# A twelve-stage perceiver block on one core: one barrier at each stage's end, the fourth couple of experts fetched by SyncE, a root ahead on ScalarE

## What is computed

```python
x = x + _L0_xattn_ref(_layernorm(x), ctx_1024, ...)     # stage slots
x = x + _L0_attn_ref(_layernorm(x), ...)                # patt
x = x + _L0_ffn_ref(_layernorm(x), ...)                 # quant
x = x + _L1_xattn_ref(_layernorm(x), ctx_1024, ...)     # padded
x = x + _L1_attn_ref(_layernorm(x), Wqkv, bqkv, Wo, bo) # folded
x = x + _L1_ffn_ref(_layernorm(x), Wg, w1, w2)          # moe
x = x + _L2_xattn_ref(_layernorm(x), ctx_1024, ...)     # cross
x = x + _L2_attn_ref(...)  # delta    then _L2_ffn_ref   # local
x = x + _L3_xattn_ref(...) # plain    then _L3_attn_ref  # mqa
x = x + _L3_ffn_ref(...)   # hashed

def _L1_attn_ref(x, Wqkv, bqkv, Wo, bo):
    qkv = (x @ Wqkv.T + bqkv).reshape(B, 16, S, 3 * hd)
    ...
def _L1_ffn_ref(x, Wg, w1, w2):
    gate = softmax(xr @ Wg); idx = argmax(gate)
    h = relu(einsum('ecm,emf->ecf', dispatched, w1))
    expert_out = einsum('ecf,efm->ecm', h, w2)
    ...
```

## Time and profile before

| | |
|---|---|
| median of 3 runs | 1777.92 us (1773.97 to 1778.31) |
| the profiled execution | 1778.89 us |
| its span, first to last instruction | 1777.1 us |
| TensorE matmul busy | 1433.1 us (81%) |
| VectorE busy | 1001.7 us (56%) |
| ScalarE busy | 700.0 us (39%) |
| GpSimd busy | 96.5 us (5%) |
| mean DMA rate over the span | 102 GB/s |

### The profile page before, as it was taken

The page is one execution under the profiler, slowest core; times in us unless marked ns, Lnnn a source line. Parts: engine busy times, 40 slices in busy tenths (PEclk is TensorE's granted clock), DMA queues, the critical chain, the costliest instruction groups (busy, mean ns, idle before and its releaser), DMA issues. The chain is left out here.

```text
span 1777.1 us, 28179 instructions
## 1 busy us (share of the span) xinstructions
PE 1433.1 (81%) x10760; PEld 1067.2 (60%) x10760; DVE 1001.7 (56%) x2900; ACT 700.0 (39%) x1524; POOL 96.5 (5%) x90
## 2 busy tenths in 40 slices
PE   7999999776598447799999999999983654647975
PEld 6979889554376233367776777777762532445763
DVE  5645444584565312277777777777756945343333
ACT  5735445212121110167667667666761010112211
POOL 2300000000000210200000000001000000000000
PEclk9999999888799659799999999999996565658997
DMA  9944333100331749410000000000002007007810
GB/s 320 327 164 160 118 111 140 53 1 20 139 131 56 249 153 350 180 59 33 33 33 33 33 33 33 33 32 33 2 1 116 1 0 301 0 0 261 277 57 4
DMA packets 61783, 181.15 MB, mean 102 GB/s; under 512 B 7249, under 2 KB 41169, under 8 KB 60369
## 3 DMA queue, kind: packets, MB, share of 16 engines
q1 hardware_dynamic: 56864, 156.77, 24.7%
q0 software_dynamic: 4352, 16.78, 2.6%
q10 hardware_dynamic: 432, 5.80, 0.8%
HBM read 178.68 MB, written 0.66 MB: 101 GB/s over the span
## 5 line engine op out<-in xcount | busy, mean ns | idle before, releaser
L1733 ACT ACTIVATE cross_s<-cross_s,cross_shift 128x896 f32<-128x896 f32 x224 | 215.1, 1031 | 35.2 <-DVE cross_shift L1813 35.2
L1727 ACT COPY cross_eT<-cross_ring 128x512 f32<-128x512 f32 x280 | 153.2, 591 | 144.9 <-PE cross_ring L1653 144.9
L1653 PE MATMUL cross_ring<-consts,cross_s 128*128 128x128 f32 x1568 | 199.4, 280 | 8.7 <-ACT cross_s L1733 8.7
L1653 PEld LDWEIGHTS cross_ring<-consts,cross_s 128*128 128x128 f32 x1568 | 170.7, 142 | 59.1 <-issue 43.8
L1804 DVE CUSTOM_DVE_ANT_0 cross_s<-cross_scores,cross_mask,cross_top 128x448 f32<-128x448 f32 x224 | 141.3, 680 | 84.3 <-PE cross_scores L1645 84.3
L374 ACT ACTIVATE slots_probs<-slots_scores,slots_bias,ctx_rinv 128x128 f32<-128x128 f32 x294 | 130.2, 460 | 109.0 <-DVE slots_bias L418 109.0
L1804 DVE CUSTOM_DVE_ANT_0 cross_s<-cross_scores,cross_mask,cross_half_max 128x448 f32<-128x448 f32 x224 | 141.3, 681 | 18.8 <-PE cross_scores L1645 18.8
L134 PE MATMUL slots_scores<-slots_qkT,slots_ctxT 128*128 128x128 f32 x1176 | 139.8, 277 | 9.1 <-DMA slots_ctxT<-in_ctxT 8.2
L134 PEld LDWEIGHTS slots_scores<-slots_qkT,slots_ctxT 128*128 128x128 f32 x1176 | 138.3, 194 | 13.0 <-DMA slots_ctxT<-in_ctxT 9.2
L324 PE MATMUL slots_attended<-ctx_rows,slots_probs 128*128 128x257 f32 x588 | 135.2, 380 | 1.4 <-DVE slots_pooled L432 1.4
L1645 PE MATMUL cross_scores<-cross_keysT,cross_qz 32*128 32x448 f32 x896 | 119.0, 589 | 0.8 <-DVE cross_keysT L1778 0.8
(11 more groups left out here) (742 smaller groups left out, 2114.3 us busy)
## 6 DMA issues: line engine op xcount, KB each, us to landing
slots_ctxT<-in_ctxT SPq DMA_DIRECT2D x42, 896.0 KB, 4.6
ctx_rows<-in_ctx_rows SPq DMA_DIRECT2D x28, 896.0 KB, 7.6
padded_ctxT<-in_ctxT SPq DMA_DIRECT2D x14, 896.0 KB, 4.6
cross_ctxT<-in_ctxT SPq DMA_DIRECT2D x14, 896.0 KB, 4.6
plain_ctxT<-in_ctxT SPq DMA_DIRECT2D x14, 896.0 KB, 4.7
ring_w<-in_moe_w POOLq DMA_DIRECT2D x12, 1024.0 KB, 17.8
ring_w<-in_moe_w SPq DMA_DIRECT2D x12, 1024.0 KB, 11.8
local_layers<-in_w_local SPq DMA_DIRECT2D x2, 4806.0 KB, 15.3
```

What stands on the lines that cost most here:

```text
L1653: last = pe.transpose(bank(("turn", u, t))[:, j * P:(j + 1) * P], s_buf[:, u % 2, j, t * P:(t + 1) * P], K.ident)
L1727: act.copy(eT[:, u % 2, t], bank(item)).then_inc(st("emptied_act"), 1)
L1733: act.activation(rows, rows, ACT.Exp, bias=shift[:, u % 2, j:j + 1], scale=SCALE).then_inc(st("exp"), 1)
```

## The change

Four edits.

- `Stage.__exit__` no longer has the second barrier. GpSimd clears the stage's semaphores while the others go on. To keep that safe, every new semaphore takes a number that is not among those just cleared (`semaphore`, `Stage.cleared`). The numbers a stage gets then lie in more than one run, so the clearing at its end is one to four instructions where it was one.
- GpSimd fetches couples 0 to 2 in the folded stage, and no longer waits for `o2_in`.
- SyncE fetches couple 3 as its first work in the moe stage.
- `root_table` is put at the end of ScalarE's list in every stage but hashed: a square root of one column of the constants into `K.unused`, which nobody reads. The load of the table with the root thus stands at the end of a stage and no longer at the start of the next.

```diff
+def semaphore(nc, name):
+    num = next(n for n in nc.free_semaphores if n not in Stage.cleared)
+    return nc.alloc_semaphore(name=name, num=num)
 class Stage:
+    cleared = []
...
-            self.sems[name] = self.nc.alloc_semaphore(name=f"{self.name}_{name}")
+            self.sems[name] = semaphore(self.nc, f"{self.name}_{name}")
...
-            self.nc.clear_and_free_semaphores(list(self.sems.values()))
-            self.nc.all_engine_barrier()
+            mine = list(self.sems.values())
+            Stage.cleared = [s.num for s in mine]
+            self.nc.clear_and_free_semaphores(mine)
...
+def root_table(act, K):
+    act.activation(K.unused, K.ident[:, 0:1], ACT.Sqrt)
...
                 softmax_scalar(act, st, "f", ef[:, :], D ** -0.5)
+                root_table(act, K)
...
             def _(pool):
                 pool.wait_ge(st("folded_in"), 16)
-                for p in range(SLOTS):
-                    if p == SLOTS - 1:
-                        pool.wait_ge(st("o2_in"), 16)
+                for p in range(SLOTS - 1):
                     K.ring.fetch_w1(pool, p)
                     K.ring.fetch_w2(pool, p)
...
             def _(sp):
+                K.ring.fetch_w1(sp, SLOTS - 1)
+                K.ring.fetch_w2(sp, SLOTS - 1)
                 for p in range(SLOTS, COUPLES):
                     sp.wait_ge(st("hid_mm"), p - SLOTS + 1)
                     K.ring.fetch_w1(sp, p)
```

More of the change, by code:

```diff
@@ L76, in __init__ @@
         self.T, self.region = T, region
-        self.arrived = {n: nc.alloc_semaphore(name=f"arrived_{n}") for n in HOMES}
+        self.arrived = {n: semaphore(nc, f"arrived_{n}") for n in HOMES}
     def buf(self, name):
@@ L946, in scalar @@
                 exponentials(g)
+        root_table(act, self.K)
     def vector(self, dve):
@@ L1251, in __init__ @@
         self.w2 = [w2[:, s] for s in range(SLOTS - 1)] + [second]
-        self.w1_in = [nc.alloc_semaphore(name=f"w1_in{n}") for n in range(2 * SLOTS)]
-        self.w2_in = [nc.alloc_semaphore(name=f"w2_in{n}") for n in range(2 * SLOTS)]
+        self.w1_in = [semaphore(nc, f"w1_in{n}") for n in range(2 * SLOTS)]
+        self.w2_in = [semaphore(nc, f"w2_in{n}") for n in range(2 * SLOTS)]
     def turn(self, p):
@@ L2225, in __init__ @@
         self.T, self.rotary, self.layers = T, rotary, layers
-        self.arrived = [nc.alloc_semaphore(name=f"arrived_local{n}") for n in range(LAYERS)]
+        self.arrived = [semaphore(nc, f"arrived_local{n}") for n in range(LAYERS)]
     def fetch(self, eng, n):
@@ L2747, in perceiver @@
         K = Kept()
-        out_written = nc.alloc_semaphore(name="out_written")
+        out_written = semaphore(nc, "out_written")
         K.x = sb("x_kept", [P, D])[:, :]
@@ L2753, in perceiver @@
         K.idle = consts[:, 0:2 * P]
+        K.unused = sb("unused", [P, 1])[:, :]
         with Stage(nc, "first") as st:
```

2 lines of the change are left out of this document (1 added, 1 removed).

## The result

| | before | change |
|---|---|---|
| median | 1775.95 us (1773.39 to 1778.31, 4 runs) | 1751.39 us (1749.61 to 1752.29, 4 runs) |
| profiled execution | 1778.89 us | 1752.29 us |
| its span | 1777.1 us | 1750.2 us |

The ratio is 0.9861, 95% interval 0.9842 to 0.9880. In the changed kernel's numbering L161 is L169, L165 is L173, L172 is L180, L1144 is L1161, L1261 and L1265 are L1277 and L1281, L1362 is L1381, L789 and L819 are L805 and L835.

A forecast was written before the change was run, and what follows sets the result against it. TensorE binds the long stages; the change touches only seams, where VectorE waits 28.7 us on the second barrier. 10.7 + 7.5 + 1.6 = 19.8 us off 1778.9 gives 1759.1 us, range 1752 to 1766.

The forecast's parts named there:

- Couple 3, 10.7 us: Folded's end: GpSimd's drain waits for its own couple 3 transfers; moving them to SyncE takes 10.7 us off.
- Both covers: In moe: couple 3 lands 14 us before TensorE wants it; SyncE is free for couple 4 with 4 us left.
- couple 3 again: Rival in moe: SyncE's four transfers delay couple 4, costing up to the 11 us gained: 1769.8, chance 0.06.
- the drain by itself: Rival at folded's end: GpSimd's DRAIN is long without waiting for transfers, so 10.7 us stay: 1769.8, chance 0.05.
- The barrier, 7.5 us: Stage ends: one barrier less, 14 times, saves 8.2 us less most of quant's part: 7.5 us.
- The first rival: Stage starts: the second barrier hid the next block's start; 3.8 us stay (1762.9), or all (1766.6); chance 0.16.
- The root, 1.6 us: Starts of folded, delta, mqa and hashed: no table load ahead of the root saves 0.39 us each, 1.6 us.
- clock can equally fall sooner somewhere: Unknown: TensorE's clock may drop earlier in some stage, losing a like amount to the 2.4 us possible in moe.
- the reading by the row: Quant: the library load runs from MODIFY_POOL_CONFIG, 7.6 us to the first call, so quant gains only 0.1 us.
- the rival's 1.1 us: Quant: load counted from L819's end, gaining 1.1 us more; in the rival "more than the sum", 1755.6, chance 0.12.
- the list of unknowns: Two unknowns: what the second barrier covered (0 to 8.2 us gained) and TensorE's clock at moe's start (0 to 2.4).
- The whole stretch at full clock, 2.4 us: Moe's start: TensorE's clock may rise sooner after a shorter pause, gaining up to 2.4 us; nothing was counted.

The follow-up runs named there:

- e1: The kernel before with only couple 3's fetch moved from GpSimd to SyncE: 1761.93 us, ratio 0.9911.
- e2: The kernel before with one barrier a stage end in place of two and the semaphores' numbers chosen as in the change: 1767.66 us, ratio 0.9937.
- e3: The kernel before with only the unused root added in ten stages, its buffer keeping all addresses modulo 64: 1772.76 us, ratio 0.9968.
- e14: The changed kernel with GpSimd's library loaded in patt and the weights' fourth place moved 184 bytes, to 0 modulo 256: 1745.44 us, ratio 0.9822.
- e0: The kernel before, unchanged, against itself: 1776.22 us against 1776.43, ratio 0.9997.
- e9: The changed kernel with GpSimd's library loaded in patt by one unused PARTITION_ALL_REDUCE: 1744.28 us, ratio 0.9818.
- e10: The kernel before with an unused buffer of 96 bytes a partition, ring_w at 64 modulo 128: 1776.38 us in one execution.
- e13: The kernel before with an unused buffer of 160 bytes a partition, ring_w at 128 modulo 256: 1774.69 us in one execution.
- e6: The kernel before with 18 products into an unused bank at the end of TensorE's list in folded: 1776.57 us, ratio 1.0002.
- e11: The kernel before with the first couples' places at 48 and the second weights' at 16 modulo 64 bytes: 1777.37 us in one execution.
- e12: The kernel before with an unused buffer of 288 bytes a partition, ring_w at 0 modulo 256: 1771.90 us in one execution.
- e5: The changed kernel with its unused buffer 64 bytes a partition, so ring_w lies modulo 64 as in the kernel before: 1759.17 us, ratio 0.9908.
- e7: The changed kernel with the fourth place of the experts' weights (couples 3 and 7) moved by 24 bytes: 1752.20 us, ratio 0.9865.
- e8: The changed kernel with the fourth place of the experts' weights (couples 3 and 7) moved by 56 bytes: 1751.77 us, ratio 0.9867.
- e4: The kernel before with an unused buffer taking 32 bytes a partition ahead of all others, no instruction changed: 1770.77 us, ratio 0.9959.

## Why the prediction was right on couple 3 and the barrier, and missed in its sum

- **Couple 3, 10.7 us: right.** 0.1 us between VectorE's drain and the release, folded 10.73 us shorter in e1. Both covers held: couple 3 landed 13.6 us after the start (14 forecast), and SyncE was free for couple 4. The rivals "couple 3 again" and "the drain by itself" fall.
- **The barrier, 7.5 us: right in size.** The ordinary waits are 0.5 to 0.6 us, forecast 0.58; the ten together lost 7.0 us, forecast 6.5. The first rival falls with e2.
- **The root, 1.6 us: right at each start, not shown in the time.** VectorE idles 0.27 us for it in place of 0.66. In folded it can't have counted as forecast: in the kernel before the heads' output waits behind GpSimd's transfers, and in e3 it lands no sooner than before (54.9 us after the start, 54.7). Hashed is shorter by the 1.3 us forecast for barrier and root, but the clock is low there for 3.4 us in place of 5.0; in e14, low for 6.8, it is 0.2 us shorter. In mqa the gain did not arrive: there TensorE's clock, low for 17.1 us before, is low for 20.5, and the stage is 0.7 us longer. In e14, where it is low for 17.1 us again, mqa is 36.96 us, the 0.9 forecast. That is the "clock can equally fall sooner somewhere".
- **Quant: the reading by the row was right.** The first call came 7.1 us after MODIFY_POOL_CONFIG. In 14 of the 15 traces with the loading in quant it comes after 7.0 to 7.3 us (7.65 in the first of the kernel before), while the gap behind the end of VectorE's row goes from 4.6 to 5.7. In e3 VectorE is 0.4 us sooner than in e0 and the call is not: 7.2 us after the configuring in both. So the loading runs from MODIFY_POOL_CONFIG and does not wait for VectorE, as the prediction's sum had it, and e9 shows that it is what the call waits for. The stage is as long as in e0 (43.41 against 43.40 us), so the rival's 1.1 us did not come. The figure of the Trainium skill's GPSIMD Engine Reference, section 2.1, 5.95 us, is that gap less the wait for the event, and this difference is no constant here (4.6 to 5.7). In patt the loading took longer, 9.8 us (e9) and 9.9 (e14).
- **What failed: the list of unknowns.** "The whole stretch at full clock, 2.4 us. I take nothing": it came, as 2.0 us to couple 4's issue (e1, e10 and e13, where the clock rises as early and no root was moved, come to the same 16.2 to 16.3 us). The reason given, that the clock had been at 0.50 before the pause too, did not bear: in e3 it rose early from 0.50, and without a shorter pause. It is late in both traces of the kernel before (9.6, 9.3 us), in e6, e11 and e12 (9.4, 12.6, 9.3), and rises 2.8 to 5.5 us after the start in the twelve other kernels, so most edits moved it. What decides is open.
- **And a term was missing.** The change was costed as instructions. Its buffer of 4 bytes was named ("into `K.unused`, which nobody reads") and costed at nothing. It moved `ring_w` to 0 modulo 256, in two places where transfers bind: 2.3 us in moe's middle part and, by e5, 1.3 in folded's output (folded as a whole came out 0.9 beyond its forecast, with the output issued 2.9 us later than before). With the address put back (e5) the median is 1759.17 us; the forecast was 1759.1. That agreement is luck in part: the interval is 4 us each way, and in e5's trace cross is 1.4 us longer than before where 0.6 less was forecast.
- The rest of the surplus, 1.6 us in cross above all, goes with the clock: in cross it fell to 0.50 for 3.4 us at 761.8 and again 563 us later in the kernel before and in e0, and neither time in the change, e1, e3, e7 or e13. The five without the two falls have a cross of 612.3 to 612.8 us, all others 614.6 to 616.4. It need not be the same in every execution of a kernel: e8's profiled one has the falls and took 1754.97 us, against a median of 1751.77. Hence the range should have had 2 to 4 us more below, for the clock alone. e1, e2, e3 and e4 gained 16.1, 10.4, 5.3 and 7.2 us, 39 together against the change's 24.6: each has the early clock in moe, which can be gained but once and is part of this, and the first three gained 3 to 5 us more than their term.

## What to carry to other kernels

GpSimd's drain at a barrier waits for the transfers that GpSimd issued, SyncE's did not: look at what GpSimd still has in flight where a block ends, and give late fetches to SyncE. Before costing an edit look at where it moves the buffers behind it, and put the destination of transfers from HBM in pieces of 1 KB at a multiple of 256 bytes. Where many short stages end at half clock, allow a few us either way for any edit, and judge a mechanism by its own row in the trace, not by the total.

## What the runs showed of the hardware that was not expected

- GpSimd's DRAIN at a barrier lasts until its own transfers have landed: it ended 0.5 us after the last landing in the change (625.6, 625.1) and 0.7 in the kernel before (648.9, 648.2). SyncE's took 0.12 us and ended 5.6 us ahead of couple 7's last landing (710.9, 716.5).
- The start of a place in SBUF modulo 256 bytes: 2.58 to 2.63 against 3.01 us for 1 MB in 1 KB pieces, 401 to 403 against 375 to 378 GB/s over eight transfers of both kinds, 381 against 342 in GpSimd's.
- TensorE's clock followed one pattern from padded on in two executions of one kernel (e0). With the same instructions and other addresses it rose in moe after 2.8 us (e4), 3.0 (e10), 3.3 (e13), 9.3 (e12) and 12.6 (e11).
- The loading of a GpSimd library function runs from MODIFY_POOL_CONFIG: in quant the first call comes 7.0 to 7.3 us after it whenever VectorE is done (one trace 7.65). Once it was loaded in patt (9.8 us, beside other work), the first call in quant came 0.1 us behind VectorE.
